# Cross attention: value units moved into their own batch's steps, context loads and opening block reordered

## What is computed

```python
qh = (q @ wq + bq).reshape(b, -1, NH, D).transpose(0, 2, 1, 3)
kh = (k @ wk + bk).reshape(b, -1, NH, D).transpose(0, 2, 1, 3)
vh = (v @ wv + bv).reshape(b, -1, NH, D).transpose(0, 2, 1, 3)
attn = jnp.einsum('bhqd,bhkd->bhqk', qh, kh) / SCALE
score = jax.nn.softmax(attn, axis=-1)
out = jnp.einsum('bhqk,bhkd->bhqd', score, vh)
out = out.transpose(0, 2, 1, 3).reshape(b, -1, NH * D)
return out @ wo + bo
```

## Time and profile before

| what | us |
|---|---|
| median of three runs | 2355.11 (2352.07 to 2359.96) |
| the profiled execution | 2351.33 |
| its span, first to last instruction | 2349.1 |
| first score of the second block | 53.25 |
| batches 1 to 14, together | 720.61 |
| last batch, first score to end of the last weighing | 65.52 |
| TensorE busy in the span | 2168.8 (92%) |
| VectorE, ScalarE, GpSimd busy | 1315.5, 997.3, 331.6 |

### The profile page before, as it was taken

How to read it: one execution, slowest core, us unless ns; L and a number is a source line. 1 busy time by engine, 2 the same in 40 slices (tenths; PEclk the granted TensorE clock), 3 DMA queues, 4 the chain that set the end, 5 groups by cost and what they waited for, 6 DMA issues and landing times. The chain is left out here.

```text
span 2349.1 us, 39843 instructions
## 1 busy us (share of the span) xinstructions
PE 2168.8 (92%) x15922; PEld 1499.2 (64%) x15922; DVE 1315.5 (56%) x2292; ACT 997.3 (42%) x1868; POOL 331.6 (14%) x366
## 2 busy tenths in 40 slices
PE   7999999999999977999998899978999999887796
PEld 4777777777777754555554677854555554545795
DVE  4566666656665634555553344447777772667554
ACT  1555555555555552333433011114666665516121
POOL 3322222232222200000000000014000000000241
PEclk9999999999999978999999899998999999898798
DMA  6877776777777521000000212113111111013312
GB/s 200 197 171 183 179 174 154 173 178 171 183 178 176 127 59 51 6 12 6 6 1 1 115 68 94 55 45 78 28 33 36 24 24 31 23 43 136 135 48 78
DMA packets 101338, 216.18 MB, mean 92 GB/s; under 512 B 58738, under 2 KB 66299, under 8 KB 95428
## 3 DMA queue, kind: packets, MB, share of 16 engines
q1 hardware_dynamic: 98420, 204.93, 35.3%
q0 software_dynamic: 2208, 6.03, 0.8%
q10 hardware_dynamic: 528, 2.69, 0.4%
HBM read 91.16 MB, written 15.20 MB: 45 GB/s over the span
## 5 line engine op out<-in xcount | busy, mean ns | idle before, releaser
L1089 DVE TENSOR_REDUCE L_xattn_maxima<-L_xattn_scores 128x1 f32<-128x1024 f32 (+1 forms) x256 | 253.6, 991 | 239.4 <-PE L_xattn_scores L1012 239.0
L1156 ACT ACTIVATE L_xattn_probs_t<-L_xattn_turned 128x1024 f32<-128x1024 f32 (+1 forms) x256 | 220.8, 862 | 332.6 <-PE L_xattn_turned L1024 332.6
L1997 DVE TENSOR_REDUCE shared_half_maxima<-shared_ring 128x1 f32<-128x578 f32 (+1 forms) x251 | 244.4, 991 | 89.9 <-PE shared_ring L1903 87.1
L2077 ACT ACTIVATE shared_exps<-shared_scores 128x512 f32<-128x512 f32 (+1 forms) x416 | 225.7, 594 | 122.6 <-PE shared_scores L1924 122.0
L1168 ACT ACTIVATE L_xattn_probs<-L_xattn_scores,L_xattn_maxima 128x1024 f32<-128x1024 f32 (+1 forms) x256 | 235.6, 925 | 37.7 <-DVE L_xattn_maxima L1092 37.7
L1024 PEld LDWEIGHTS L_xattn_turned<-ident,L_xattn_probs 128*128 128x128 f32 x1664 | 197.3, 144 | 79.7 <-issue 46.7
L1024 PE MATMUL L_xattn_turned<-ident,L_xattn_probs 128*128 128x128 f32 x1664 | 233.9, 280 | 12.9 <-ACT L_xattn_probs_t L1156 12.0
L686 PE MATMUL L_xattn_projected<-L_xattn_wv,L_xattn_ctx 128*128 128x256 f32 x780 | 193.0, 389 | 0.0
L680 PE MATMUL L_xattn_projected<-L_xattn_ctx,L_xattn_wk 128*128 128x400 f32 x480 | 182.0, 501 | 0.0
L1012 PE MATMUL L_xattn_scores<-L_xattn_k_stack,L_xattn_q_stack 128*128 128x512 f32 (+1 forms) x512 | 159.0, 392 | 22.2 <-ACT L_xattn_probs L1168 11.0
L1924 PE MATMUL shared_scores<-shared_q,shared_k 128*128 128x512 f32 (+1 forms) x416 | 154.1, 449 | 0.1
(11 more groups left out here) (392 smaller groups left out, 3152.7 us busy)
## 6 DMA issues: line engine op xcount, KB each, us to landing
L_xattn_k_stack<-L_xattn_k_part SPq DMA_DIRECT2D x504, 200.2 KB, 4.3
L_xattn_ctx<-in_ctx_t SPq DMA_DIRECT2D x16, 1602.0 KB, 7.0
ffn_task<-in_ffn_task SPq DMA_DIRECT2D x16, 1024.0 KB, 6.7
experts_w_in<-in_expert_in SPq DMA_DIRECT2D x8, 1024.0 KB, 11.5
shared_k<-k_scratch SPq DMA_DIRECT2D x64, 100.1 KB, 3.3
L_xattn_q_stack<-q_scratch SPq DMA_DIRECT2D x128, 32.0 KB, 2.0
k_scratch<-L_xattn_shared_part SPq DMA_DIRECT2D x128, 32.0 KB, 1.7
shared_q<-q_scratch SPq DMA_DIRECT2D x64, 64.0 KB, 3.6
```

The source lines that it names most:

```text
L1089: nc.vector.reduce_max(maxima[n % 2][:, half:half + 1], cols, axis=AX).then_inc(halves_maxed, 1)
L1156: nc.scalar.activation(probs_t[:, t:t + m, p * P:(p + 1) * P], turned_tiles[:, 0:m, :], ACT.Copy).then_inc(turned_moved, 1)
L1997: nc.vector.reduce_max(half_maxima[:, n, half:half + 1], found[:, 0:HALF_STARTS[half + 1] - HALF_STARTS[half]], axis=AX).then_inc(ring_max ...
L2077: nc.scalar.activation(exps[n % 2][0:m, h * BANK:(h + 1) * BANK], scores[0:m, h, :], ACT.Exp, scale=SCALE).then_inc(exps_done, 1)
```

## The change

The value units of a batch leave the steps of the batch before, and the opening block, and go into the batch's own steps 0 to 4. A step now has three places: after the first half-score, right after the second, and after the five transposes. The first holds a value unit (or, in step 5, the shared unit of b + 1), the second the key unit of b + 1, the third the second value unit where a step has two (steps 0 and 2), or the turn unit (step 7). Steps 6 and 7 have nothing in the first place. The last batch keeps its own value units. SP loads the context of batch b + 2 in step 4, when the last value unit of b is projected, ahead of the second group's stacks, and stores the shared parts after them. The opening block loads the context of batch 0 in four pieces, projects its first key units among the transposes and query units, leaves out the values, and issues half of `load_q` from ScalarE.

```diff
-    odd_units = [("shared", 0)] + [("values", i) for i in range(V_UNITS)]
-    units = [unit for i in range(K_UNITS) for unit in (("keys", i), odd_units[i])] + [("turn", 0)]
-    U = len(units)
+    first_units = [("keys", i) for i in range(K_UNITS)] + [("shared", 0), ("turn", 0)]
+    VALUES_OF_STEP = ((0, 1), (2,), (3, 4), (5,), (6,), (), (), ())
+    SHARED_STEP = GROUP_PAIRS + 1
+    places = []
+    for n in range(PAIRS):
+        values = [(0, ("values", i)) for i in VALUES_OF_STEP[n]]
+        places += [values[:1] + ([(1, ("shared", 0))] if n == SHARED_STEP else []), [(1, ("keys", n))],
+                   values[1:] + ([(1, ("turn", 0))] if n == PAIRS - 1 else [])]
...
-                    sp.dma_start(wk[:], dram[f"{layer}_wk"]).then_inc(keys_loaded, 16)
-                    load_ctx(sp, 0, 0)
+                    sp.dma_start(wk[:], dram[f"{layer}_wk"]).then_inc(keys_loaded, 16)
+                    load_columns(0)
...
+                    load_columns(1)
                     sp.dma_start(wq[:], dram[f"{layer}_wq"]).then_inc(query_loaded, 16)
...
-                    load_q(sp, 0, 0)
+                    load_q(sp, 0, 0, range(0, COPIES // 2))
...
+                    act.wait_ge(query_stored, 16 * 2 * len(q_units))
+                    load_q(act, 0, 0, range(COPIES // 2, COPIES))
                     act.wait_ge(keys_split, CHUNKS_PER_GROUP)
...
-                        if n == GROUP_PAIRS - 1:
-                            store_shared(sp, b + 1)
+                        if n == GROUP_PAIRS - 1 and ctx_left:
+                            sp.wait_ge(projection_done, order_of(b, ("values", V_UNITS - 1)) + 1)
+                            load_ctx(sp, b + 2, parity)
+                    store_shared(sp, b + 1)
                     if q_left:
                         load_q(sp, b + 2, parity)
-                    if ctx_left:
-                        sp.wait_ge(projection_done, U * (b + 2))
-                        load_ctx(sp, b + 3, 1 - parity)
...
+                def fill(b, i, last):
+                    for ahead, unit in places[i]:
+                        if ahead == 1 and last:
+                            continue
+                        project(pe, b + ahead, unit, projected[:, 0], order_of(b + ahead, unit))
+
...
                         score(b, parity, n, 0)
-                        if not last:
-                            project(pe, b + 1, 1 - parity, 2 * n, projected[:, 0], U * (b + 1) + 2 * n)
+                        fill(b, 3 * n, last)
...
                         score(b, parity, n, 1)
-                        if not last:
-                            project(pe, b + 1, 1 - parity, 2 * n + 1, projected[:, 0], U * (b + 1) + 2 * n + 1)
+                        fill(b, 3 * n + 1, last)
...
-                        if n == PAIRS - 1 and not last:
-                            project(pe, b + 1, 1 - parity, U - 1, projected[:, 0], U * (b + 1) + U - 1)
+                        fill(b, 3 * n + 2, last)
```

More of the change, by code:

```diff
@@ L575, in cross_attention_block, with order_of @@
     V_UNITS = len(v_units)
-    odd_units = [("shared", 0)] + [("values", i) for i in range(V_UNITS)]
-    units = [unit for i in range(K_UNITS) for unit in (("keys", i), odd_units[i])] + [("turn", 0)]
-    U = len(units)
-    assert U == 2 * PAIRS + 1
+    first_units = [("keys", i) for i in range(K_UNITS)] + [("shared", 0), ("turn", 0)]
[6 more added lines that the diff above has]
+                   values[1:] + ([(1, ("turn", 0))] if n == PAIRS - 1 else [])]
+    slots = [slot for place in places for slot in place]
+    U, FIRST_UNITS = len(slots), len(first_units)
+    last_slots = [slot for slot in slots if slot[0] == 0]
+    def order_of(b, unit):
+        if b == 0 and unit in first_units:
+            return first_units.index(unit)
+        if (0, unit) in slots:
+            return FIRST_UNITS + U * b + (slots if b < BATCH - 1 else last_slots).index((0, unit))
+        return FIRST_UNITS + U * (b - 1) + slots.index((1, unit))
     with ExitStack() as stack:
@@ L616, in load_ctx, with load_q @@
             sp.dma_start(ctx[parity][:], dram["ctx_t"][ds(b, 1)].rearrange("o p c n -> (o p) c n")).then_inc(ctx_loaded[parity], 16)
-        def load_q(sp, b, parity):
-            for copy in range(COPIES):
+        def load_q(sp, b, parity, copies=range(COPIES)):
+            for copy in copies:
                 for e in range(2):
@@ L654, in split_shared @@
         def split_shared(pool, b):
[L655 removed]
+            pool.wait_ge(projection_moved, order_of(b, ("shared", 0)) + 1)
             if b > 0:
@@ L663, in split_parts @@
         def split_parts(pool, b):
-            for what, i in units:
+            for what, i in first_units if b == 0 else [unit for ahead, unit in slots if ahead == 1]:
                 if what == "keys":
@@ L668, in split_parts, with project @@
                     split_shared(pool, b)
-        def project(pe, b, parity, u, bank, moved):
-            if u == 0:
-                pe.wait_ge(ctx_loaded[parity], 8 * (b - parity) + 16)
+        def project(pe, b, unit, bank, moved):
+            parity = b % 2
+            what, n = unit
+            if what == "keys" and n == 0 and b > 0:
+                pe.wait_ge(ctx_loaded[parity], 8 * (b + parity))
             if moved > 0:
                 pe.wait_ge(projection_moved, moved)
-            what, n = units[u]
             if what == "keys":
@@ L700, in project, with move_projection @@
             last.then_inc(projection_done, 1)
-        def move_projection(dve, b, parity, u, bank):
-            dve.wait_ge(projection_done, U * b + u + 1)
-            what, n = units[u]
+        def move_projection(dve, b, unit, bank):
+            parity = b % 2
+            what, n = unit
+            dve.wait_ge(projection_done, order_of(b, unit) + 1)
             if what == "keys":
@@ L752, in first_block @@
             keys_loaded = core.sem(first, f"{layer}_keys_loaded")
+            columns_loaded = [core.sem(first, f"{layer}_columns_loaded{i}") for i in range(CHUNKS_PER_GROUP)]
+            shared_loaded = core.sem(first, f"{layer}_shared_loaded")
             values_loaded = core.sem(first, f"{layer}_values_loaded")
@@ L812, in _, with project_first @@
                 def _(pe):
+                    def project_first(u):
+                        what, n = first_units[u]
+                        if what == "keys" and n < CHUNKS_PER_GROUP:
+                            pe.wait_ge(columns_loaded[n], 16)
+                        if what == "shared":
+                            pe.wait_ge(shared_loaded, 32)
+                        project(pe, 0, first_units[u], banks[:, u % 4], max(u - 3, 0) if what != "turn" else u)
+                    pe.wait_ge(keys_loaded, 32)
+                    pe.wait_ge(bank_ready, 1)
+                    project_first(0)
                     pe.wait_ge(ident_loaded, 16)
@@ L821, in _ @@
                             last.then_inc(x_turned_ready, 1)
-                    def project_first(u):
-                        if u == 0:
-                            pe.wait_ge(keys_loaded, 16 * 4)
-                            pe.wait_ge(bank_ready, 1)
-                        if units[u] == ("values", 0):
-                            pe.wait_ge(values_loaded, 16)
-                        project(pe, 0, 0, u, banks[:, u % 4], max(u - 3, 0) if units[u][0] != "turn" else u)
-                    for u in range(EARLY):
-                        project_first(u)
+                        if t == TILES // 2 - 1:
+                            project_first(1)
                     pe.wait_ge(query_loaded, 32)
                     for i, (m, half) in enumerate(q_units):
+                        if i == CHUNKS:
+                            project_first(2)
                         pe.wait_ge(x_turned_moved, half + 1)
@@ L1119, in keep_heads, with move_place @@
                                             ALU.add).then_inc(heads_ready, 1)
+                def move_place(b, i, last):
+                    for ahead, unit in places[i]:
+                        if ahead == 1 and last:
+                            continue
+                        move_projection(dve, b + ahead, unit, projected[:, 0])
                 def batch(b, parity, first, last):
```

51 lines of the change are left out of this document (26 added, 25 removed).

## The result

The changed kernel takes 2417.8 us in the median of four runs (2416.7 to 2428.59); the kernel before 2357.05 in four (2352.07 to 2359.96). The ratio over all these runs is 1.0267, with a 95% interval of 1.024 to 1.0295 (the two medians alone give 1.0258): 2.7% slower. The median is 2.2 us under the 2420 forecast.

The account below looks back on a forecast made before the run. TensorE bounds the stage only because each step's units just fill the gaps of two chains. Opening -8.5, fifteen batches +72.2 (+4.81 each), last batch +0.9: +64.6 on 2351.33, plus 3.8, gives 2420 us; range 2401 to 2446.

Parts of the forecast that it names:

- Units change halves: Step 1 to 2: key unit in half A leaves its 2.94 us, value unit lengthens half B; 6.09 against 5.62, +0.47.
- Two value units in a step: Steps 0 to 1 and 2 to 3: units sharing one bank wait for VectorE's moves; +2.32 us each.
- The floor of light steps: Key-only steps 5 to 6 and 6 to 7 fall to the bare step's 5.08 us, not 3.61; -0.54 each.
- The opening: Opening block without seven value units: loads start earlier, first score comes 8.5 us sooner; bounds -5 and -11.
- The first step: From the first score to the first second half-score: no difference forecast, 0 us.
- The last batch: Seven value units enter its bare steps, costing and gaining nothing there; with the step into it, together +0.9 us.
- The context load: On SP after the first group's four stacks: lands in 7.0 us median with 3.3 us of cover, costing nothing.
- The 3.8 us added for the median: Profiled execution before, 2351.33 us, lies 3.8 under the median of three runs, 2355.11; added back to the sum.

Follow-up runs that it names:

- second kernel: Changed kernel with key units after the first half-score and first value units after the second, both two-value steps kept; 2429.64 us, ratio 1.0335.

## Why the prediction was right

The number is right, and its largest term for the reason given. By step, from the second half-scores of the fifteenth batch (831.97, 843.27, 849.27, 857.33, 862.47, 871.70, 876.78, 881.86, 888.34):

| step to step | forecast | measured |
|---|---|---|
| 0 to 1 (two values, weighing) | 11.18 | 11.30 |
| 1 to 2 | 6.09 | 6.00 |
| 2 to 3 (two values) | 7.94 | 8.06 |
| 3 to 4 (short value) | 5.18 | 5.14 |
| 4 to 5 (shared, weighing) | 9.37 | 9.23 |
| 5 to 6, 6 to 7 (key only) | 5.08 each | 5.08 each |
| 7 to the next | 6.33 | 6.48 |

**Units change halves**: shown. The wait for the exponentials appears where a key unit took the value unit's place (0.46), and the kernel with the halves swapped and nothing doubled loses 2.65 us a batch.

**Two value units in a step**: shown, 2.5 us for each by taking away first one and then both. The parts of it are as put: waits of 0.18 and 0.33 for VectorE's moves, and for the rest the unit's own length, which nothing is left to hide.

**The floor of light steps**: shown, 5.08 with a key unit as without, and it moves with VectorE's maximum. A point I did not make: with keys first the light steps take 5.62 and the single ones 5.62 as well (second kernel), so the swap of halves by itself changes next to nothing in this table (56.44 against 56.36), because it also empties half B of the light steps. The two causes do not add up: from the change as made, undoing the swap alone saves nothing a batch, undoing the doubled steps alone saves 2.3, and undoing both saves the whole 4.9. With keys first the two doubled steps cost 5.0; the swap costs 2.65 only where every half is full. My sum has both terms in it and comes out right, but a reader who took +0.47 a step for an avoidable part of this change's loss would be wrong.

**The opening**: the mis-sized term, -12.4 for -8.5, beyond the bound of -11. The split of the fourth key unit ended at 28.33 (forecast 28.6). What failed is that I took the same bytes for the same time and let the second queue save nothing. In the kernel before, SP issued all eight query loads and then its eight stacks, and ended 14.1 us after the split (51.44 - 37.30), while ScalarE's queue issued the other eight stacks meanwhile:

```profile
37.33 6.83 ACTq L629 DMA_DIRECT2D L_xattn_k_stack<-L_xattn_k_part  x8
```

```profile
37.19 5.95 SPq L622 DMA_DIRECT2D L_xattn_q_stack<-q_scratch  x8
43.18 8.26 SPq L629 DMA_DIRECT2D L_xattn_k_stack<-L_xattn_k_part  x8
```

With the query loads shared as well, both queues are through 10.7 us after the split. These 3.5 us, the 0.3 by which the split came sooner than in my table (8.97 for 8.7), and the 0.2 that I had rounded off make up the missing 3.9. Timeline of both queues and the first score in the changed kernel:

```profile
28.15 1.82 ACTq L640 DMA_DIRECT2D L_xattn_q_stack<-q_scratch  x4
30.01 8.99 ACTq L647 DMA_DIRECT2D L_xattn_k_stack<-L_xattn_k_part  x8
```

```profile
28.16 1.74 SPq L640 DMA_DIRECT2D L_xattn_q_stack<-q_scratch  x4
29.94 8.56 SPq L647 DMA_DIRECT2D L_xattn_k_stack<-L_xattn_k_part  x8
39.66 3.57 SPq L654 DMA_DIRECT2D k_scratch<-L_xattn_shared_part  x8
```

```profile
40.84 1.19 PE L1044 MATMUL L_xattn_scores<-L_xattn_k_stack,L_xattn_q_stack 128*128 128x512 f32 x2 [6.23 <-DVE L_xattn_fold L1180]
```

**The first step**: +1.0, where the forecast had nothing. A value unit stands there, at half clock (3.62), where a key unit of 2.62 stood.

**The last batch**: +3.2 for +0.4. Its first five steps take 10.56, 7.67, 7.32, 5.14 and 9.53, where I had 10.63, 6.09, 7.39, 5.18 and 8.11. The clock fell to half in step 2, which lengthens the second of them, and again in the weighing of the fifth. A value unit took 3.44 there, for 1.89 to 1.99 elsewhere. Timeline of TensorE:

```profile
902.51 3.44 PE L704 MATMUL L_xattn_projected<-L_xattn_wv,L_xattn_ctx 128*128 128x256 f32 x8
...
923.24 4.42 PE L1071 MATMUL L_xattn_weighed<-L_xattn_probs_t,L_xattn_v 128*32 128x128 f32 x104 [0.57 <-issue]
```

The value units cost nothing there, as I had it; that the clock would stay up among them was wrong. This 2.8, the 1.0 of the first step and 0.5 in the fifteen batches nearly cancel the opening's 3.9. That 65.1 matches 64.6 so closely is luck: the sum is better than its terms.

**The context load**: right, it costs nothing. The loads land 8.2 us after their issue in the median (8.7 at most), where I had 7.0. SP issued the last one at 819.74, and the key unit that wants it starts at 832.3, some 4 us after even the latest landing. The kernel with one unit in each half and keys first wants it earlier, and still has batches of 51.42.

**The 3.8 us added for the median** rest on nothing that was shown: the medians differ by 60.8, the attentions in the two traces by 65.1. What makes the difference of 4 is open; a single stretch at half clock in the later stages, as above, is worth more than that.

## What to carry to other kernels

A stage in which TensorE is 98% busy can still be bound by a chain in one half of each step. Look at what releases each half and at TensorE's own part in it, and fill the half that a chain holds open with the longest unit, the other with the shortest. Total work that stays the same is no argument for the same time: a crowded step pays in full, and an emptied one gives back only what lies above the chain's floor. Before a block is shortened, ask which DMAs its length covered: here a wait of 5.8 us came out on VectorE, and one order of two units kept 3.8 us of it out of the path where the other did not.

## What the runs showed of the hardware that I had not expected

The granted clock falls to half for a moment in step 6 of five batches of the kernel that has the key unit in half B there and two waits of 0.94 and 0.75 us in half A, and in four batches of the kernel with one doubled step, whose step 6 is the same. In the changed kernel, with waits of 0.46 and 0.61 (rows above), it falls in none but the last batch, there too after waits of 0.94 and 0.75. But the same step keeps the clock in the other ten and eleven batches, so the waits are at most a part of the cause. Such a fall costs 1.7 us (58.1 for 56.44).

The Trainium skill (TensorE: Matmul & The Clock Gate, Part 4: PE-mode transpose) says that transposes do not count as busy for the clock as matmuls do. The half before the fall held a score, five transposes (0.74) and 1.69 of idle time, so the trace fits it but does not show it: no run here separates transposes from idle time.

In four kernels with key units first, one early batch is 1.4 to 2.2 us longer than its neighbours (52.93 for 51.42 in the one with one unit a half) with the clock up. In that one eight transposes start, and seven of them come late, with nothing that the timeline shows to wait for:

```profile
286.07 0.33 PE L1063 MATMUL L_xattn_turned<-ident,L_xattn_probs 128*128 128x128 f32 x1
287.70 0.93 PE L1063 MATMUL L_xattn_turned<-ident,L_xattn_probs 128*128 128x128 f32 x7 [1.31 <-issue]
```

Such idle times, 0.6 to 1.7 us, stand eleven times in the batches of six traces, always in the weighing or the eight transposes of step 5; the kernel with the new opening alone and the kernel before with short maxima have them too, the changed kernel none. Before each of the eleven, TensorE resumes 2.4 to 2.9 us after a transfer of 16 KB starts in the DMA queue that the profile names "instruction" (284.83 for the 287.70 above), and about 55 such transfers fall in the fifteen batches. So a late supply of instructions is the likely cause; no run tests it.

One stretch at half clock in the second attention made the profiled execution of the changed kernel 9.3 us longer against the kernel before, in code that is the same. Its three other executions, with spans 10 to 12 us shorter, have a mean clock of 0.961 to 0.962 where it has 0.955, which fits the same cause.
